# Mamba stage: the rows of C split into three bf16 parts on GpSimd and spread over the partitions by one bf16 matmul

## What is computed

```python
xz = x @ W_in + b_in
x_proj, z = jnp.split(xz, 2, axis=-1)
xa = silu(conv(x_proj, conv_k) + conv_b)
dtBC = xa @ W_xp + b_xp
dt_int, B_c, C_c = jnp.split(dtBC, [DT_RANK, DT_RANK + D_STATE], axis=-1)
dt = softplus(dt_int @ W_dt + b_dt)
A = -exp(A_log)
def step(h, inp):
    x_t, dt_t, B_t, C_t = inp
    h = exp(dt_t[..., None] * A) * h + dt_t[..., None] * B_t[:, None, :] * x_t[..., None]
    y_t = jnp.sum(C_t[:, None, :] * h, axis=-1)
    return (h, y_t)
_, y = jax.lax.scan(step, h0, (xa, dt, B_c, C_c))
y = y + xa * D_ssm
return y * silu(z) @ W_out + b_out
```

## Time and profile before

| | |
|---|---|
| time, median of 3 runs | 5653.92 us |
| lowest, highest | 5646.5, 5664.32 us |
| the profiled execution's own time | 5647.35 us |
| its span in the trace | 5645.6 us |
| busy in the span | PE 90%, PEld 61%, DVE 70%, ACT 59%, POOL 46% |
| the Mamba stage in the span | about 59 to 681 us |

### The profile page before, as it was taken

How to read it: one execution, slowest core, us unless ns; L and a number is a source line. 1 busy time by engine, 2 the same in 40 slices (tenths; PEclk the granted TensorE clock), 3 DMA queues, 4 the chain that set the end, 5 groups by cost and what they waited for, 6 DMA issues and landing times. The chain is left out here.

```text
span 5645.6 us, 131981 instructions
## 1 busy us (share of the span) xinstructions
PE 5086.0 (90%) x50825; PEld 3436.4 (61%) x50825; DVE 3933.9 (70%) x6558; ACT 3357.5 (59%) x5891; POOL 2606.1 (46%) x1596
## 2 busy tenths in 40 slices
PE   7999855799799999999999999999999999899897
PEld 4445423465477767776777677767776677566544
DVE  4888789677577777776777677767777777567553
ACT  3555422355466766776666666766676677545434
POOL 2555411000266556655666566656655555366300
PEclk8999865799899999999999999999999999999899
DMA  2111000000000010001000100010001000000020
GB/s 61 60 60 60 34 0 0 7 2 2 28 12 11 11 32 12 11 11 32 12 11 11 32 12 11 11 32 12 11 11 32 12 11 11 16 2 2 23 61 19
DMA packets 75523, 113.01 MB, mean 20 GB/s; under 512 B 21888, under 2 KB 52816, under 8 KB 71440
## 3 DMA queue, kind: packets, MB, share of 16 engines
q1 hardware_dynamic: 67040, 109.78, 7.0%
q10 hardware_dynamic: 8256, 0.03, 0.1%
HBM read 69.56 MB, written 2.49 MB: 13 GB/s over the span
## 5 line engine op out<-in xcount | busy, mean ns | idle before, releaser
L2199 POOL TENSOR_TENSOR lt_qk<-lt_qk,lt_rot 128x1024 f32<-128x1024 f32 x384 | 908.3, 2365 | 223.7 <-DVE lt_rot L2562 223.7
L2209 POOL TENSOR_TENSOR lt_prob<-lt_prob,lt_total 128x1024 f32<-128x1024 f32 x192 | 365.4, 1903 | 1083.1 <-DVE lt_total L2584 1083.1
L2204 POOL TENSOR_TENSOR lt_qk<-lt_qk,lt_rnorm 128x1024 f32<-128x1024 f32 x384 | 727.3, 1906 | 113.1 <-ACT lt_rnorm L2438 105.6
L2246 PE MATMUL lt_ps<-lt_w_qk,lt_xs 128*128 128x512 f32 x1536 | 746.5, 609 | 36.2 <-issue 23.2
L2297 PE MATMUL lt_ps<-lt_z,lt_fold 128*128 128x256 f32 x3072 | 678.9, 379 | 1.3 <-ACT lt_z L2466 1.2
L2297 PEld LDWEIGHTS lt_ps<-lt_z,lt_fold 128*128 128x128 f32 x3072 | 583.5, 190 | 121.9 <-ACT lt_z L2466 25.0
L2559 DVE TENSOR_TENSOR lt_qk<-lt_ps,lt_table 128x1024 f32<-128x1024 f32 x384 | 468.0, 1219 | 95.1 <-ACT lt_sq L2428 86.7
L2562 DVE TENSOR_TENSOR lt_rot<-lt_ps,lt_table 128x512 f32<-128x512 f32 x768 | 490.3, 679 | 0.0
L2574 DVE TENSOR_REDUCE lt_nmax<-lt_ps 128x16 f32<-128x1024 f32 x192 | 229.4, 1195 | 366.0 <-PE lt_ps L2265 366.0
L2569 DVE TENSOR_REDUCE lt_norm<-lt_sq 128x16 f32<-128x1024 f32 x384 | 463.6, 1207 | 0.0
L2246 PEld LDWEIGHTS lt_ps<-lt_w_qk,lt_xs 128*128 128x128 f32 x1536 | 272.5, 193 | 264.7 <-issue 259.7
(11 more groups left out here) (400 smaller groups left out, 10132.2 us busy)
## 6 DMA issues: line engine op xcount, KB each, us to landing
mb_bs<-mb_rows SPq DMA_DIRECT2D x16, 1536.0 KB, 7.5
lt_xw<-lt_xw SPq DMA_DIRECT2D x192, 128.0 KB, 2.3
mb_bs<-mb_rows SPq DMA_DIRECT2D x16, 512.0 KB, 4.2
mo_gate_b<-mo_rows SPq DMA_DIRECT2D x16, 512.0 KB, 5.6
lt_xs<-h SPq DMA_DIRECT2D x96, 64.0 KB, 1.9
lt_w_qk<-in_L_ffn_Wqkv SPq DMA_DIRECT2D x6, 1024.0 KB, 5.1
lt_xs<-h SPq DMA_DIRECT2D x96, 63.8 KB, 1.9
lt_wvT<-in_L_wvT SPq DMA_DIRECT2D x6, 512.0 KB, 7.3
```

The source lines that it names most:

```text
L2199: pool.tensor_tensor(qk[:, u, :, :], qk[:, u, :, :], rot[:, u % 2, :, :], ALU.add).then_inc(sg["added"], 1)
L2204: pool.tensor_tensor(qk[:, u, :, :], qk[:, u, :, :], rnorm[:, u, :, :].to_broadcast([P, H, DH]), ALU.mult).then_inc(sg["qk"], 1)
L2246: last = pe.matmul(AT[u][:, 512 * k:512 * k + 512], xs[:, m.j, c:c + P], w_qk[:, a, 512 * k:512 * k + 512], start=True, stop=True)
```

## The change

The selection matrix now has 112 rows, in which the 16 rows of the identity stand three times (at rows 0, 64 and 96), and is kept as bf16. `w_xp` and `b_xp` have the columns of C three times, so that the projection gives C at rows 0, 64 and 96 of `bcd`, with B at 16 and dt at 32. In group 4 GpSimd writes `parts` = bf16(bcd) for all 112 rows and `rest` = bcd - parts for rows 64 to 111, in group 5 the second part bf16(rest) for rows 64 to 111 and the third part rest - second for rows 96 to 111. `spread` is then one bf16 matmul for each state over all 112 rows; its first one in an item waits for the third part (`c_low`) instead of `bcd`. The rows of B and dt meet zero rows of the selection matrix.

```diff
-    out["mamba_sel"] = np.repeat(np.eye(N2, dtype=f32)[:, :, None], P, axis=2)
+    N = T["L0_attn_A_log"].shape[1]
+    out["mamba_sel"] = np.zeros((112, N, P), f32)
+    for row in (0, 64, 96):
+        out["mamba_sel"][row:row + N] = np.eye(N, dtype=f32)[:, :, None]
...
-    ROW_C, ROW_DT = 32, 64
+    ROW_HIGH, ROW_B, ROW_DT, ROW_MID, ROW_LOW = 0, 16, 32, 64, 96
+    ROWS = ROW_LOW + N
...
-        sel = sb("sel", [ROW_C + N, N, P])
+        sel = sb("sel", [ROWS, N * P], BF16)
...
+        parts = sb("parts", [ROWS, 2, S], BF16)
+        rest = sb("rest", [ROWS, S])
...
-        LOADS = 15
+        LOADS = 19
+        staged = bs[0:ROWS, 0, 0, 0:N * P // S, :].rearrange("p n s -> p (n s)")
...
-            sp.dma_start(w_xp[:, :, 0:N], w_bc[:, :, R:R + N]).then_inc(sg["w_in"], 16)
-            sp.dma_start(w_xp[:, :, ROW_C:ROW_C + N], w_bc[:, :, R + N:R + 2 * N]).then_inc(sg["w_in"], 16)
-            sp.dma_start(w_xp[:, :, ROW_DT:], w_bc[:, :, 0:R]).then_inc(sg["w_in"], 16)
-            sp.dma_start(sel[ROW_C:, :, :], T["mamba_sel"][N:2 * N, N:2 * N, :]).then_inc(sg["w_in"], 16)
+            sp.dma_start(w_xp[:, :, ROW_B:ROW_B + N], w_bc[:, :, R:R + N]).then_inc(sg["w_in"], 16)
+            for row in (ROW_HIGH, ROW_MID, ROW_LOW):
+                sp.dma_start(w_xp[:, :, row:row + N], w_bc[:, :, R + N:R + 2 * N]).then_inc(sg["w_in"], 16)
+            sp.dma_start(w_xp[:, :, ROW_DT:ROW_DT + R], w_bc[:, :, 0:R]).then_inc(sg["w_in"], 16)
+            sp.dma_start(staged, T["mamba_sel"].rearrange("r n p -> r (n p)")).then_inc(sg["w_in"], 16)
...
+            pool.tensor_copy(sel[:, :], staged).then_inc(sg["sel"], 1)
...
             def phase(n, j, g):
+                if g == 4:
+                    pool.wait_ge(sg["bcd"], n + 1)
+                    wait(pool, sg["c_spread"], G * (n - 1))
+                    pool.sem_inc(sg["split_step"], 1)
+                    pool.tensor_copy(parts[:, j, :], bcd[:, j, :]).then_inc(sg["c_high"], 1)
+                    pool.wait_ge(sg["c_high"], n + 1)
+                    wait(pool, sg["c_low"], n)
+                    pool.tensor_tensor(rest[ROW_MID:, :], bcd[ROW_MID:, j, :], parts[ROW_MID:, j, :],
+                                       ALU.subtract).then_inc(sg["c_rest"], 1)
+                    pool.wait_ge(sg["c_rest"], n + 1)
+                if g == 5:
+                    wait(pool, sg["drive"], G * (n - 1) + g + 2)
+                    pool.sem_inc(sg["split_step"], 1)
+                    pool.tensor_copy(parts[ROW_MID:, j, :], rest[ROW_MID:, :]).then_inc(sg["c_mid"], 1)
+                    pool.wait_ge(sg["c_mid"], n + 1)
+                    pool.tensor_tensor(parts[ROW_LOW:, j, :], rest[ROW_LOW:, :], parts[ROW_LOW:, j, :],
+                                       ALU.subtract).then_inc(sg["c_low"], 1)
+                    pool.wait_ge(sg["c_low"], n + 1)
                 if g == 6:
...
+            pe.wait_ge(sg["sel"], 1)
...
             def spread(n, j, g):
                 if g == 0:
-                    pe.wait_ge(sg["bcd"], n + 1)
+                    pe.wait_ge(sg["c_low"], n + 1)
                 wait(pe, sg["read"], G * n + g)
                 for k in range(2):
-                    last = pe.matmul(ps_n[:, 0, k, :], sel[ROW_C:, 2 * g + k, :], bcd[ROW_C:ROW_C + N, j, :], start=True, stop=True,
-                                     tile_position=(ROW_C, 0))
+                    last = pe.matmul(ps_n[:, 0, k, :], sel[:, P * (2 * g + k):P * (2 * g + k) + P], parts[:, j, :], start=True, stop=True)
                 last.then_inc(sg["c_spread"], 1)
```

## The result

The changed kernel takes 5597.0 us (median of four runs, 5595.3 to 5599.79) against 5652.51 us for the kernel before (5646.5 to 5664.32); the ratio is 0.9902, with a 95% interval of 0.9889 to 0.9915. That is 55 us less, where 30 were forecast, and under the range of 5603 to 5649 us. The profiled execution has a span of 5593.5 us, 52.1 less than before. First the page: its span, and the busy time of each engine.

A forecast was written before the change was run, and what follows sets the result against it. TensorE's stretch preparing the next item was taken as the bound: 27.3 us from fourteen items plus 3 from item 0, about 30, with split and loads 0 and clock unchanged, gave 5624 us from 5653.92; range 5603 to 5649.

The forecast's parts named there:

- The bound and the direct gain: TensorE's preparation stretch in groups 1 to 3 bounds; the cheaper spread saves 1.95 us an item, 27.3 us over fourteen.
- The stall before scan(4): VectorE's wait behind ScalarE's decay(4), 1.18 us before; a sign of being right was growth to some 2 us.
- I take the two to cancel: 1.4 us as before: TensorE's clock falls in almost every item, but each us at half clock costs less; loss stays 1.4 us an item.
- `read` waited 18.1 us for `ps_n`, not 30: Sign of being right: VectorE's read waits some 30 us in place of 74 for the spread rows.
- the items came under 34.5 us: Sign of being right: gatings of y in the Mamba stage 34.5 to 35.5 us apart.
- The ends of the stage: Item 0, at half clock, gains 3 us from the cheaper spread; the last item prepares nothing and gains 0.
- The split on GpSimd: Four instructions an item, 2.5 us at most, hidden in GpSimd's gaps; cost 0, or 37 us over 15 items without cover.
- the fourth case: The lighter TensorE keeps or regains its clock: items near 33.7 us, 50 us less, 5603 us; chance 0.10.
- The slower case: TensorE's clock stays at 1.2 GHz through preparation groups 1 to 3: 5679 us, or 5750 with all of it; chance 0.07.
- the one with the worst clock item: Every item pays the clock loss of the worst, 3.07 us: 36.79 us an item, 5646 us, no change; chance 0.19.
- The loads and the wider projection: 112 weight columns and more DMA at the start: 0, at most 0.1 us an item and 1 us once.

The follow-up runs named there:

- rows80: The kernel before with its fp32 spread run over all 80 rows of bcd against zero-padded selection rows, without row position, split or bf16; 5607.8 us, ratio 0.9924.
- late_out: The changed kernel with the previous item's output projection moved from group 1 to group 5 and the residual in group 7; 5626.4 us, ratio 0.9954.
- pad5: The changed kernel with each bf16 spread matmul issued five times to the same place; 5632.1 us, ratio 0.9961.
- rows80_3: The kernel before with its fp32 spread over all 80 rows of bcd and the first spread matmul issued twice; 5641.1 us, ratio 0.9986.
- before_fill: The kernel before with four throwaway fp32 matmuls of 256 columns put into TensorE's long wait of group 6; 5617.3 us, ratio 0.9939.
- after_fill: The changed kernel with six throwaway fp32 matmuls of 256 columns put into TensorE's long wait of group 6; 5605.2 us, ratio 0.9911.
- early: The changed kernel with all four split instructions on GpSimd in group 4, ahead of drive(6), instead of two each in groups 4 and 5; 5593.7 us, ratio 0.9898.
- split_alone: The changed kernel with the split kept but unused, its spread left in fp32 from row 0 of bcd; 5667.8 us, ratio 1.0023 to the kernel before.

## Why the prediction was wrong

**The bound and the direct gain were right.** The prediction's stretch from the gating of y to scan(4) was 328.56 - 312.05 = 16.51 us before and is 304.82 - 290.17 = 14.65 us now: 1.86 us saved, 1.95 forecast. Within it small errors cancel. The pair costs 0.22 us and not 0.30, and the sum behind each spread is 0.10 us cheaper, which I had not seen; rows80 shows that this and 0.20 us of the pair came from the 16 rows at a row position, not from fp32. Against that, the sum of group 0 now waits 0.21 us for the gating of y. Spread(1) stands 0.14 us behind the gating (290.31 - 290.17) where it stood 0.51 us behind it (312.56 - 312.05), 0.37 us earlier where I had 0.43, and from it to spread(3) are 300.71 - 290.31 = 10.40 us in place of 11.99. The stall before scan(4) rose to 2.01 us behind decay(4), as forecast. The Trainium skill's figure ("TensorE: Matmul & The Clock Gate", Back-to-back issue gap), 0.22 us for the pair, was the better price, and the trace agrees with it: 0.22 us.

**The step that failed is the clock: "I take the two to cancel: 1.4 us as before".** After the change the falls cost 34.12 - 34.04 = 0.08 us an item. I was right that the clock would fall in almost every item; it falls twice in most. But I set the price of a fall from those of before, and took for granted that the falls would stay of that kind. Two things changed.

The short falls became free. A fall of 3.4 us in group 7 cost 1.0 us before and costs nothing now, at nearly the same distance behind the gating (29.8 and 28.1 us). A group of spread and sum held 2.88 us of TensorE work and now holds 1.94, in 3.45 us, so what the lower clock delays is made up before the preparation groups. late_out shows the other side: in those groups the same 3.4 us are paid in full, 1.69 us. The cost of a fall is not its length, but what part of the delay reaches the stretch that bounds the kernel.

The long falls, which made 15 of the 21.8 us, nearly ceased: one of 6.8 us is left of four, and none of 10.2. I had not asked what makes a fall long. The runs narrow it (pad5 and rows80_3 have none either), but the cause stays open.

Together that is 1.5 us x 14 = 21 us of the miss. It is also in good part why `read` waited 18.1 us for `ps_n`, not 30 (in before_fill the clock alone takes this wait from 74.3 to 62.8 us), and why the items came under 34.5 us.

**The ends of the stage were the same mistake.** I gave item 0 3 us and the last item 0. They gave 7.4 and 3.3 us. before_fill gains 4.3 and 3.3 us there by the clock alone, with the spread untouched. (Item 0 of the changed kernel still holds 1.1 us that after_fill takes off, so of its 7.4 us the clock gave 3.2 to 4.3.)

**The split on GpSimd cost what was not counted.** Its own time was near (0.40 and 0.67 us an instruction, 2.1 us for the four; 0.62 each and 2.5 forecast) and hidden, `c_low` late only for item 0, 1.5 us. The miss is on VectorE, where I had put it at nothing: drive(7), 0.45 us later, lies over 0.73 us of the dt sum in place of 0.36, which costs 0.34 us an item, 5 us in all, and early took it back. I had asked who waits for the pushed instruction, and not what runs beside it.

The sum comes out: spread 1.86 x 14 + 3.1 (item 0) = 29.1 us, clock 1.5 x 14 + 4.3 + 3.3 = 28.6 us, dt sum - 0.35 x 14 = - 4.9 us; together 52.8 us, 52.2 measured in the stage. Of the rivals, the size of the fourth case came true, 0.10 by my chances, and its reason did not: the clock was not kept. The slower case and the one with the worst clock item needed falls that reach the preparation groups; the falls just behind the gating in late_out and the 10 us falls in split_alone are of that kind. The loads and the wider projection were hidden, as forecast.

## What to carry to other kernels

- A fall of TensorE's clock has to be priced by where it lies and by how much TensorE work stands around it. Walk through one item at the lower clock and see how much of the delay reaches TensorE's bound stretch; filling a wait with throwaway matmuls measures it in one run, and here took 29 us off the stage on its own.
- Before a small matmul at a row position is recast in another type, try it over more rows with zero weights: here that alone gave 45 of 55 us.
- When work is added to GpSimd, look at what VectorE runs beside everything that it pushes back, not only at who waits for it.
- Where the whole time swings by more than the effect, as here behind the stage, measure the effect between two marks in the trace.

## What the runs showed of the hardware

- An fp32 pair of 256 columns on 16 rows took 1.06 us from start to start, at row position 32 (before) and at 0 (split_alone), and the sum behind it (two fp32 matmuls of 512 columns) 1.82 us. With the pair on 80 rows and no position it took 0.86 us and the sum 1.72 us (rows80).
- A bf16 pair of 256 columns on 112 rows took 0.22 us, and the sum behind it 1.72 us.
- Falls of TensorE's clock to 0.50 followed waits of 2.15 us in the kernel before. A fall of 3.4 us cost 1.69 us where TensorE had no pause (late_out) and nothing where a group held 1.94 us of its work in 3.45 us (the change).
- Two VectorE instructions with both inputs in SBUF waited out GpSimd's drive: the dt sum ended 0.55 us behind the end of the drive that it overlapped (0.92 us with 0.36 us of overlap, 1.28 us with 0.73), the residual 0.28 us behind it (1.54 us with 1.26 us of overlap, 1.21 us with 0.93; 0.48 us with none, and the same with 0.19).
- GpSimd's price hardly depended on the number of partitions or on bf16 in or out: a subtraction of 256 columns took 0.67 us on 48 and on 16 partitions, a cast 0.40 us on 112 and on 48.
